# Criss-cross attention: more buffers for the first batch's energies, and four loads moved in the DMA queue

## What is computed

```python
q = jnp.einsum('oc,bchw->bohw', Wq, x) + bq[None, :, None, None]
k = jnp.einsum('oc,bchw->bohw', Wk, x) + bk[None, :, None, None]
v = jnp.einsum('oc,bchw->bohw', Wv, x) + bv[None, :, None, None]
energy_H = jnp.einsum('bchw,bcgw->bhwg', q, k) - NEG * eye
energy_W = jnp.einsum('bchw,bchv->bhwv', q, k)
att = softmax(concatenate([energy_H, energy_W], axis=-1), axis=-1)
out = gamma * (einsum(v, att_H) + einsum(v, att_W)) + x
```

## Time and profile before

| what | value |
|---|---|
| time, median of 3 (lowest, highest) | 4050.99 us (4048.87, 4056.91) |
| the profiled execution | 4051.03 us |
| its span | 4049.3 us |
| PE busy | 3870.5 us (96%) |
| DVE, ACT, POOL busy | 60%, 41%, 15% |
| mean granted TensorE clock | 0.979 of full speed |
| DMA moved | 874.33 MB, mean 216 GB/s |

### The profile page before, as it was taken

How to read it: one execution, slowest core, us unless ns; L and a number is a source line. 1 busy time by engine, 2 the same in 40 slices (tenths; PEclk the granted TensorE clock), 3 DMA queues, 4 the chain that set the end, 5 groups by cost and what they waited for, 6 DMA issues and landing times.

```text
span 4049.3 us, 72640 instructions
## 1 busy us (share of the span) xinstructions
PE 3870.5 (96%) x28440; PEld 3839.0 (95%) x28440; DVE 2429.3 (60%) x5084; ACT 1667.5 (41%) x3658; POOL 624.2 (15%) x793
## 2 busy tenths in 40 slices
PE   5689999999999999999999999999999999999999
PEld 5679999999999999999999999999999999999999
DVE  4454677446773566745676467754667446783544
ACT  4452445424444244442444334542445424444111
POOL 0131003200042000310013100221003210031000
PEclk7799999999999999999999999999999999999999
DMA  4376775867758777687767777677775867759665
GB/s 138 104 200 203 256 251 185 233 212 240 243 180 229 224 245 230 195 222 232 244 219 209 214 242 241 213 218 211 249 242 188 234 209 250 240 180 238 199 201 172
DMA packets 256803, 874.33 MB, mean 216 GB/s; under 512 B 34256, under 2 KB 108496, under 8 KB 256464
## 3 DMA queue, kind: packets, MB, share of 16 engines
q1 hardware_dynamic: 256464, 869.67, 69.3%
HBM read 661.92 MB, written 207.62 MB: 215 GB/s over the span
## 4 chain that ended last, share of the span: by engine, by line
PE 90%; DMA 4%; DVE 4%; issue 1%; ACT 1%; POOL 0%; SPq 0%; DVEq 0%; ACTq 0%; POOLq 0%
PE bank L890 38%; PE bank L859 16%; PE bank L878 16%; PE bank L808 11%; PE bank L818 3%; PE bank L845 3%; PE bank L827 3%; DMA Pe<-e_scratch 2%; DMA XA<-in_x 1%; DMA out<-Y 1%; DVE Sx L590 1%; DVE E L609 1%; DVE mx L604 1%; DVE zs L618 0%; DVE Sy L595 0%
## 5 line engine op out<-in xcount | busy, mean ns | idle before, releaser
L890 PE MATMUL bank<-Sy,Wv_hi 128*128 128x384 f32 x6144 | 1595.1, 340 | 11.9 <-DVE Sy L595 11.9
L890 PEld LDWEIGHTS bank<-Sy,Wv_hi 128*128 128x128 f32 x6144 | 1087.9, 188 | 13.1 <-issue 13.1
L890 PE MATMUL bank<-Sy,Wv_lo 128*128 128x384 f32 x3072 | 1029.0, 335 | 0.0
L675 DVE SCALAR_TENSOR_TENSOR Y<-bank,bv_sb,Y 128x384 f32<-128x384 f32 x768 | 472.0, 615 | 872.2 <-PE bank L890 871.7
L878 PE MATMUL bank<-Pt,XT_r 128*128 128x96 f32 x6144 | 725.9, 275 | 15.6 <-DVE Y L666 9.4
L372 POOL TENSOR_TENSOR Pe<-Pe,F 96x384 f32<-96x384 f32 x384 | 319.3, 834 | 2701.8 <-DMA Pe<-e_scratch 2668.2
L878 PEld LDWEIGHTS bank<-Pt,XT_r 128*128 128x128 f32 x6144 | 705.6, 192 | 18.8 <-DVE Y L666 11.0
L496 ACT ACTIVATE Sy<-Y 128x768 fp32r<-128x768 f32 x384 | 302.8, 835 | 834.6 <-PE bank L890 799.8
L658 DVE COPY Y<-bank 128x96 f32<-128x96 f32 x1536 | 317.6, 321 | 499.3 <-PE bank L859 499.3
L890 PEld LDWEIGHTS bank<-Sy,Wv_lo 128*128 128x128 f32 x3072 | 576.8, 188 | 0.0
L808 PE MATMUL bank<-Sx,Wqk_hi 128*128 128x384 f32 x1536 | 425.0, 359 | 74.4 <-DVE Sx L590 74.4
(11 more groups left out here) (52 smaller groups left out, 3015.5 us busy)
## 6 DMA issues: line engine op xcount, KB each, us to landing
XA<-in_x SPq DMA_DIRECT2D x192, 768.0 KB, 5.4
Y<-in_x SPq DMA_DIRECT2D x192, 768.0 KB, 6.0
XT_r<-in_x_row SPq DMA_DIRECT2D x384, 384.0 KB, 5.4
out<-Y SPq DMA_DIRECT2D x192, 768.0 KB, 3.6
XT_r<-in_x_col SPq DMA_DIRECT2D x192, 384.0 KB, 4.8
XT_c<-in_x_col SPq DMA_DIRECT2D x192, 384.0 KB, 4.8
e_scratch<-E SPq DMA_DIRECT2D x384, 144.0 KB, 2.6
Pe<-e_scratch SPq DMA_DIRECT2D x384, 144.0 KB, 6.2
```

The source lines that it names most:

```text
L675: nc.vector.scalar_tensor_tensor(at, proj_ps[c % 2][:, 0:CP], bv_sb[:, c:c + 1], at, op0=ALU.add, op1=ALU.add).then_inc(out_made, 1)
L890: last = nc.tensor.matmul(proj_ps[c % 2][:, 0:CP], w[:, ct, at], Sy[:, lo, ct, :], start=(ct == 0 and k == 0), stop=(ct == CT - 1 and k == 2))
```

## The change

Four things are changed. In the prologue there are two buffers of split x (Sx and Sx_first, by turns) and four of raw x (XA and XA_first), and SP issues the loads of four chunks before it stores anything. DVE prepares Wv after the row energies, no longer ahead of the second chunk. In the column stage, SP issues one XT_c piece, then `load_p` of group 3, then the two other XT_c pieces; `load_xres(b, 0)` now comes after the loads of group 12. In the row stage, the next batch's first two XA loads are issued in iteration 4.

```diff
+            XA_first = sb("XA_first", [P, 2, CT, CP], F32, s2)
+            Sx_first = sb("Sx_first", [P, 2, CT, CP], F32R, s2)
...
+        def xa(a, m):
+            return XA_first[:, m % 4 - 2, :, :] if a == 0 and m % 4 >= 2 else XA[:, m % 2, :, :]
+
+        def sx(a, m):
+            return Sx_first if a == 0 and m % 2 else Sx
...
+            def load_xa_first(m):
+                if m >= 4:
+                    sp.wait_ge(x_lo_made, past(x_lo_made, (m - 3) * HALVES))
+                sp.dma_start(xa(0, m).rearrange("p t n -> p (t n)"), x[0, m, :, :]).then_inc(xa_first_in[m % 4], 16)
...
             def column_stage(b):
-                for i in range(RRING, CRING):
+                load_xtc(b, RRING)
+                load_p(b, PRING)
+                for i in range(RRING + 1, CRING):
                     load_xtc(b, i)
-                load_xres(b, 0)
                 for g in range(CHUNKS):
-                    load_p(b, g + PRING)
+                    if g:
+                        load_p(b, g + PRING)
...
+                    if g == CHUNKS // 2:
+                        load_xres(b, 0)
...
-                    if more and n + 1 == A_FIRST:
+                    if more and n + 2 == A_FIRST:
                         load_xa(b + 1, 0)
                         load_xa(b + 1, 1)
...
                     if h == 0:
-                        act.wait_ge(x_half_used, past(x_half_used, a * CHUNKS + m))
+                        act.wait_ge(x_half_used, past(x_half_used, a * CHUNKS + m + 1 - turns(a)))
                     else:
-                        act.wait_ge(qk_summed, past(qk_summed, a * CHUNKS + m))
+                        act.wait_ge(qk_summed, past(qk_summed, a * CHUNKS + m + 1 - turns(a)))
...
                 low_x(0, 0)
+                for m in range(CHUNKS):
+                    if m + 1 < CHUNKS:
+                        low_x(0, m + 1)
+                    shift(0, m, before=False)
+                    if m:
+                        sum_z(0, m - 1)
+                sum_z(0, CHUNKS - 1)
                 dve.wait_ge(wv_in, 16)
                 nc.vector.tensor_copy(Wv_hi[:, :, :], raw_v[:, :, :]).then_inc(w_hi_made, 1)
```

More of the change, by code:

```diff
@@ L81, in criss_cross_attention @@
         with ExitStack() as s2:
-            sb("below_raw", [P, 16, CT, CP], F32, s2)
+            sb("below_first", [P, 12, CT, CP], F32, s2)
+            XA_first = sb("XA_first", [P, 2, CT, CP], F32, s2)
+            Sx_first = sb("Sx_first", [P, 2, CT, CP], F32R, s2)
             raw_v = sb("raw_v", [P, CT, C], F32, s2)
@@ L132, in criss_cross_attention @@
         xa_in = [sem(f"xa_in{j}") for j in range(2)]
+        xa_first_in = [sem(f"xa_first_in{j}") for j in range(4)]
         x_hi_made, x_lo_made, x_half_used = sem("x_hi_made"), sem("x_lo_made"), sem("x_half_used")
@@ L150, in criss_cross_attention @@
         out_stored = [sem(f"out_stored{j}") for j in range(2)]
-        by_dma = (*xa_in, *e_stored, *p_in, *xtc_in, *xtr_in, *xres_in, *out_stored)
+        by_dma = (*xa_in, *xa_first_in, *e_stored, *p_in, *xtc_in, *xtr_in, *xres_in, *out_stored)
         by_pe = (x_half_used, qk_summed, e_summed, p_turned, o_summed, proj_summed)
@@ L192, in _, with load_xa @@
                 sp.sem_inc(s, START[s])
-            def load_xa(a, m, before=True):
-                j = m % 2
+            def load_xa(a, m):
                 if m >= 2:
                     sp.wait_ge(x_lo_made, past(x_lo_made, (a * CHUNKS + m - 1) * HALVES))
-                elif before:
+                else:
                     out_landed(sp, a - 1, m)
-                sp.dma_start(XA[:, j, :, :].rearrange("p t n -> p (t n)"), x[a, m, :, :]).then_inc(xa_in[j], 16)
+                sp.dma_start(XA[:, m % 2, :, :].rearrange("p t n -> p (t n)"), x[a, m, :, :]).then_inc(xa_in[m % 2], 16)
+            def load_xa_first(m):
+                if m >= 4:
+                    sp.wait_ge(x_lo_made, past(x_lo_made, (m - 3) * HALVES))
+                sp.dma_start(xa(0, m).rearrange("p t n -> p (t n)"), x[0, m, :, :]).then_inc(xa_first_in[m % 4], 16)
             def store_row_energies(a, m):
@@ L308, in prologue @@
                 sp.dma_start(raw_qk[:, :, :], wqk_t.rearrange("(t p) n -> p t n", p=P)).then_inc(wqk_in, 16)
-                load_xa(0, 0, before=False)
+                load_xa_first(0)
                 sp.dma_start(bqk_sb[:, :], bqk).then_inc(small_in, 16)
@@ L312, in prologue @@
                 sp.dma_start(bv_sb[:, :], bv).then_inc(small_in, 16)
-                load_xa(0, 1, before=False)
+                for m in range(1, 4):
+                    load_xa_first(m)
                 sp.dma_start(raw_v[:, :, :], wv_t.rearrange("(t p) n -> p t n", p=P)).then_inc(wv_in, 16)
                 for m in range(CHUNKS):
-                    if m + 2 < CHUNKS:
-                        load_xa(0, m + 2)
+                    if m + 4 < CHUNKS:
+                        load_xa_first(m + 4)
                     if m:
@@ L438, in _, with round_x @@
                 act.sem_inc(s, START[s])
[L440 to L445, removed]
+            def round_x(a, m):
+                if a == 0:
+                    act.wait_ge(xa_first_in[m % 4], past(xa_first_in[m % 4], 16 * (m // 4 + 1)))
+                else:
+                    act.wait_ge(xa_in[m % 2], past(xa_in[m % 2], 16 * ((a - 1) * (CHUNKS // 2) + m // 2 + 1)))
+                    if m == 0:
+                        for slot in SX_SLOTS:
+                            out_landed(act, a - 1, slot)
                 for h, cts in enumerate(halves):
                     if h == 0:
-                        act.wait_ge(x_half_used, past(x_half_used, a * CHUNKS + m))
+                        act.wait_ge(x_half_used, past(x_half_used, a * CHUNKS + m + 1 - turns(a)))
                     else:
-                        act.wait_ge(qk_summed, past(qk_summed, a * CHUNKS + m))
-                    nc.scalar.activation(Sx[:, 0, cts, :], XA[:, j, cts, :], ACT.Copy).then_inc(x_hi_made, 1)
+                        act.wait_ge(qk_summed, past(qk_summed, a * CHUNKS + m + 1 - turns(a)))
+                    nc.scalar.activation(sx(a, m)[:, 0, cts, :], xa(a, m)[:, cts, :], ACT.Copy).then_inc(x_hi_made, 1)
             def evict_kq(a, m, before=True):
@@ L553, in prologue @@
                 nc.scalar.activation(Wqk_hi[:, :, :], raw_qk[:, :, :], ACT.Copy).then_inc(w_hi_made, 1)
-                round_x(0, 0, before=False)
+                round_x(0, 0)
                 act.wait_ge(small_in, 48)
@@ L589, in low_x @@
                     dve.wait_ge(x_hi_made, past(x_hi_made, (a * CHUNKS + m) * HALVES + h + 1))
-                    nc.vector.tensor_tensor(Sx[:, 1, cts, :], XA[:, m % 2, cts, :], Sx[:, 0, cts, :].bitcast(F32),
-                                            ALU.subtract).then_inc(x_lo_made, 1)
+                    nc.vector.tensor_tensor(sx(a, m)[:, 1, cts, :], xa(a, m)[:, cts, :],
+                                            sx(a, m)[:, 0, cts, :].bitcast(F32), ALU.subtract).then_inc(x_lo_made, 1)
             def low_y(b, n, h):
@@ L766, in prologue @@
                 dve.wait_ge(gbv_made, 1)
[L767 to L773, removed]
                 for g in range(CHUNKS):
@@ L807, in project_kq @@
                     for n, (w, lo) in enumerate(((Wqk_hi, 0), (Wqk_hi, 1), (Wqk_lo, 0))):
-                        last = nc.tensor.matmul(ps[:, 0:CP], w[:, ct, :], Sx[:, lo, ct, :],
+                        last = nc.tensor.matmul(ps[:, 0:CP], w[:, ct, :], sx(a, m)[:, lo, ct, :],
                                                 start=(ct == 0 and n == 0), stop=(ct == CT - 1 and n == 2))
```

## The result

The changed kernel takes 4032.37 us (median of 5, 4029.24 to 4036.25) against 4051.02 us before in the same runs: a ratio of 0.995, with a 95% interval of 0.9937 to 0.9963. It is 18.7 us faster; 41 were forecast, and the time lies 0.4 us above the upper end of the range. A later set of runs, beside 13 of the kernel before, gave 4035.15 us and 0.9949 (0.9931 to 0.9966).

The account below looks back on a forecast made before the run. PE, busy 96% of the span, was taken as the bound, its idle time setting the end. Wv 3.6 + heads 33 - Y 7 + XA 11 = 40.6 us off 4051.03 gave 4010 us, range 3990 to 4032.

Parts of the forecast that it names:

- The double buffers: First energies: second Sx and four XA are no link of the chain, so 0 us for 22 chunks.
- rival 1: First energies: row energies are freed, 4.4 us a chunk instead of 7.1, 62 us gained, 3948 us; chance 0.03.
- XA: Row stage: loads an iteration earlier remove PE's 9.4 us of waits and one fallen clock, +11 us (8 to 12).
- The heads: Column-stage starts, seven boundaries: group 3's Pe ahead of Y cuts 57 us to 15 pause plus 9 clock, +33 us.
- Wv: Prologue: moving Wv gains 5.3 us at the second chunk, costs 1.7 at the column energies, net +3.6 (0 to 5).
- Y in the middle of the stage: Column stage, group 16: Y delays the Pe behind it, 0.9 us a batch, 7 us in all (0 to 34).
- Rival 2: Column-stage boundaries: clock falls behind every new pause, 21 us and not 9, 4022 us; chance 0.12.
- Rival 4: Column stage: DMAs bound it, pauses stay at the boundaries and at Y, slower at 4075 us; chance 0.04.
- Rival 3: Column stage: the queue catches up before group 4 and at Y, no pause left, 3979 us; chance 0.08.

Follow-up runs that it names:

- e6: Changed kernel with one buffer of split x in the first energies, raw x buffers and Wv's place kept: 4033.12 us, ratio 0.9961.
- e5: Changed kernel with the next batch's first two XA loads issued in row-stage iteration 5 again: 4047.45 us, ratio 0.9983.
- e1: Kernel before with only Y's chunk 0 load moved to mid column stage, ahead of group 16's Pe: 4056.84 us, ratio 1.0009.
- e4: Changed kernel with DVE making the rest of x of chunk m+2 before chunk m's maximum and subtraction: 3965.18 us, ratio 0.9772.
- e9: Changed kernel with DVE preparing Wv ahead of the second chunk's rest of x again: 4040.07 us, ratio 0.9961.
- e2: Changed kernel with Y's chunk 0 loaded in four 192 KB DMAs, after the loads of groups 1, 4, 7 and 10: 4011.3 us, ratio 0.9888.
- e3: Changed kernel with SP issuing each group's Pe one group earlier, ahead of the previous group's two pieces: 3979.34 us, ratio 0.9809.
- e7: Changed kernel with Y's chunk 0 loaded at the column stage's head again, group 3's Pe still ahead of XT_c 4 and 5: 4034.19 us, ratio 0.9957.

## Why the prediction was wrong

**What held.** The double buffers: 0 us forecast, and e6 shows 0 for the second buffer of split x. The two further buffers of raw x were not taken away in any run; no link of the row chunks' chain is a DMA, so nothing there points to them. The chain of the row energies is unchanged, and rival 1 is excluded at this order. XA: 11 us forecast, 11.5 in the rest of the two profiles, with the spread that e5 shows. The heads: the cost before was put at 57 us and measures 57.3. What would be left was put at pauses of 2.1 us in the mean and 9 us of clock, 24 in all; group 4 pauses for 1.5 to 2.3 us in the seven batches, 13.4 us together, and the heads cost 27.4 (33.4 in the second profile). So the pauses were put 1 to 2 us too high and what comes behind them 5 us too low; 33 us were forecast and 30 came, 24 in the second profile.

**Wv.** +3.6 forecast, 5.7 came. PE does not wait at all for the second chunk: the 24 matmuls of the first two chunks are one piece of the chain of waits.

```profile
9.24 6.23 PE bank L828 x24
```

The second chunk starts at 13.2 us; 13.4 was said. One matmul takes 0.34 us in it, where those of the first chunk took 0.52, and so did most of the second chunk's before the change: it runs at full rate from its start, which the sum did not have. So DVE has its first row energies 6.9 us earlier than before (16.19 for 23.14) and its last 8.9 earlier (176.48 for 185.37). The price at the column energies was higher than the 1.7 us forecast: DVE starts on them at 184.62, without a gap behind Wv, 6.7 us earlier than in the earlier trace rows. Another 1.0 us goes further on, where DVE waits for energies to be stored before it can write the next. So 2.1 us more came than was forecast, from errors of both signs.

```profile
184.62 0.55 DVE L624 TENSOR_REDUCE mx<-bank 96x4 f32<-96x384 f32 x1
```

**The step that failed is Y in the middle of the stage.** It was put at 0.9 us a batch and 7 us in all. It costs 25.4 us here, 32 in the second profile, 31.6 in e1 and 31 to 34 in e4, e5, e6 and e9. Of the 18.8 us by which the profile missed the sum (40.6 forecast, 21.8 seen), this term alone is 18.4. The place, the group and the mechanism were right; the size was off by a factor of four, from three errors that all point one way.

```profile
770.44 0.37 SPq L256 DMA_DIRECT2D Y<-in_x  x1
770.91 0.37 SPq L229 DMA_DIRECT2D Pe<-e_scratch  x1
...
778.10 0.82 POOL L390 TENSOR_TENSOR Pe<-Pe,F 96x384 f32<-96x384 f32 x1 [6.05 <-DMA Pe<-e_scratch]
```

First, this timeline shows the Pe issued 0.47 us after Y: the issue of Y itself takes SP's time. The turn was due at 778.98 - 1.18 = 777.80, 6.9 us behind the request and not 7.2, so the slack was 1.3 us, not 1.6. Second, Y holds the Pe up for longer than the 2.3 to 2.9 us that two rates from other places gave. The Pe is scaled 7.2 us after its issue in this batch and 9.1 in the fourth (issued 1737.03, scaled from 1746.15), and it landed 0.1 us before that, where the median was 4.7: 2.4 to 4.3 us more, 3.3 in the mean of the eight. The windows around the fourth batch's pause (columns as in the earlier trace rows) have the DMA engines busy the whole time at 285 and 240 GB/s. That is less than the 339 GB/s of the earlier trace rows, a stretch in which two loads of x chunks were on their way beside a store, pieces of XT_r and a Pe; why the rate differs, no run here isolates.

```profile
1739.00:1744.00 5.00, 4.93 (x46) 4.77 (x44) 2.48 (x12) 2.15 (x11) 0.00 (x0) 1.00 1.03 285
1744.00:1749.00 5.00, 1.98 (x11) 1.98 (x12) 0.00 (x0) 1.27 (x5) 0.82 (x1) 0.81 1.03 240
```

So a pause is 1.2 to 3.1 us and the eight with their followers are some 17 us, not 7. Third, the clock was left out of the forecast's value there, and no reason was given. The remaining 9 us (26.6 less 17) are mainly groups at the lower clock behind such pauses: the last window has 0.81, and the one from 1747 to 1751 has 0.57. The bound given for this term, 34 us, does hold what was measured. The value was taken from its lower end, though both ends were known; with the upper end the same sum gives 4037, above the range for the whole time (up to 4032). Of the 22 us between the forecast of 4010 and the measured time this term is the greater part.

**The rivals.** Rival 2, the clock falling behind the new pauses, came in part: it fell behind some at the head and some in the middle. What the heads cost beyond their pauses is 14 us, between the forecast's 9 and this rival's 21. The Trainium skill (TensorE: Matmul & The Clock Gate, HAM oscillation) tells of a kernel whose clock fell in each wait for a DMA; here it did not in each. Rival 4, a stage bound by its bytes, is excluded by e2 and e3, which move the same bytes and lose 5.0 and 0.5 us in the middle. Rival 3 came true only in e3, by another route: not a queue that catches up, but a request made a group earlier.

## What to carry to other kernels

A small transfer with a deadline should be asked for as soon as its buffer is free. If it stands in the queue's list behind a load that waits for something later, it loses its slack, and then any large transfer moved in front of it comes through as a pause. Moving the large one only moves the pause (e1, e7); splitting it (e2) or asking for the small one earlier (e3) removes it. Buffers do nothing while an in-order engine's list closes the loop: follow each engine's order around once before counting on them. And a term whose bounds are 0 and 34 us is not a term of 7.

## What the runs showed of the hardware

The length of a pause does not tell whether the clock falls. Behind 2.30 us a turn took 0.53 us and the granted clock stayed at 1.00; behind 1.90 us it took 0.88 and the clock was 0.50, in two batches of one execution (the timeline in the first section, and the windows behind the two turns here).

```profile
731.00:735.00 4.00, 4.00 (x40) 4.00 (x38) 1.66 (x8) 1.44 (x6) 0.82 (x1) 1.00 1.05 253
1212.00:1216.00 4.00, 4.00 (x21) 4.00 (x20) 0.81 (x4) 0.85 (x4) 0.82 (x1) 0.50 0.84 222
```
A DMA of 144 KB that landed in 4.7 us in the median took 7.1 to 9.0 us with 768 KB in front of it. Double-buffering is recommended by the Trainium skill (Trainium Kernel Development and Optimization, Best Practices); the runs have a second buffer of split x at 0 us in one order of DVE's list (e6), and at 67 us together with another order (e4).
